# Selection in the first and last pass of a graph network kernel: selectors against a PSUM column, and in the last pass message forming shared between VectorE and ScalarE

## The reference, cut to what matters

```
x = layernorm(x + L0(x))   # (1+eps)*x + segment_sum(relu(x[src] + edge_attr), dst)
x = layernorm(x + L1(x))   # two rounds of segment_sum(w * x[dst], src), w = dinv[src]*dinv[dst]
x = layernorm(x + L2(x))   # two graph convolutions: segment_sum(x[src], dst) @ w_rel + x @ w_root + b
x = layernorm(x + L3(x))   # relu(segment_sum(edge_weight * (x @ w)[src], dst) + b)
```

## Time and profile before

| | us |
|---|---|
| median of three runs | 9893.8 (9879.71 to 9897.39) |
| the profiled execution, its device time | 9887.35 |
| the profiled execution, its span | 9885.6 |
| VectorE busy | 7177.8 (73%) |
| TensorE matmul busy | 7068.5 (72%) |
| GpSimd busy | 4237.3 (43%) |
| ScalarE busy | 3856.5 (39%) |

### The profile page before, as it was taken

One profiled execution on the slowest core, in us unless ns is written; L12 is line 12 of the kernel. 1 busy time (PEld: TensorE's weight loads), 2 busy tenths in 40 slices (PEclk: granted clock), 3 DMA queues, 4 the chain that ended last, 5 costly groups with the idle time before them and its releaser, 6 DMA issues.

```text
span 9885.6 us, 235117 instructions
## 1 busy us (share of the span) xinstructions
PE 7068.5 (72%) x71829; PEld 5632.3 (57%) x71830; DVE 7177.8 (73%) x13458; ACT 3856.5 (39%) x11229; POOL 4237.3 (43%) x3907
## 2 busy tenths in 40 slices
PE   9888887878821778985666566656676666677987
PEld 8665555556611667883346335533564345566887
DVE  6655555555545778998888888888887888777996
ACT  0355555555522675435840683068206830000000
POOL 0477777777731662003630562056204620465000
PEclk9855555565555555556889788878887889555555
DMA  9466666653367996445888788868876888355442
GB/s 331 125 179 179 178 191 180 182 139 79 79 191 253 301 312 191 111 108 183 306 293 281 252 304 292 267 233 304 293 251 216 304 291 269 128 194 187 112 108 68
DMA packets 1133195, 2087.05 MB, mean 211 GB/s; under 512 B 391662, under 2 KB 655086, under 8 KB 1132590
## 3 DMA queue, kind: packets, MB, share of 16 engines
q1 hardware_dynamic: 812062, 1195.55, 41.9%
q0 software_dynamic: 219008, 627.65, 16.5%
q10 hardware_dynamic: 101904, 261.43, 7.9%
HBM read 1191.46 MB, written 892.68 MB: 211 GB/s over the span
## 4 chain that ended last, share of the span: by engine, by line
DVE 28%; issue 25%; DMA 15%; PE 14%; POOL 13%; DVEq 3%; ACT 2%; POOLq 0%; SPq 0%; ACTq 0%
POOL edge_rows L470 13%; DVE WORK L1097 7%; PE psum L818 5%; DMA WORK<-parts_by_slot 5%; DMA BIG<-edge_rows 5%; DVE WORK L1163 4%; DVE BIG L1148 4%; DVE WORK L1158 3%; PE psum L699 3%; DVE WORK L907 3%; DMA WORK<-blocks_by_edge 3%; DMA edge_rows<-WORK 2%; DVE WORK L1099 2%; ACT WORK L627 2%; PE psum L813 1%
## 5 line engine op out<-in xcount | busy, mean ns | idle before, releaser
L497 POOL DMA_INDIRECT messages_in_parts<-WORK,goal x1480 | 1437.3, 971 | 2756.8 <-ACT WORK L627 2435.7
L470 POOL DMA_INDIRECT edge_rows<-WORK x1664 | 1959.9, 1178 | 863.0 <-issue 491.1
L627 ACT CAST WORK<-psum 128x432 bf16<-128x432 f32 (+1 forms) x4440 | 1707.1, 1019 | 872.2 <-PE psum L813 872.0
L813 PE MATMUL psum<-BIG,WORK 128*128 x11840 | 1357.9, 245 | 874.3 <-DVE WORK L1097 393.9
L1097 DVE TENSOR_TENSOR WORK<-WORK,psum 128x1024 bf16<-128x1024 uint8 x1480 | 1690.3, 1213 | 358.2 <-PE psum L813 268.2
L813 PEld LDWEIGHTS psum<-BIG,WORK 128*128 128x128 bf16 x11840 | 806.8, 106 | 1425.2 <-issue 1108.2
L907 DVE TENSOR_TENSOR WORK<-lane_k,slot_part 128x1024 bf16<-128x1024 bf16 x2220 | 1509.5, 680 | 8.6 <-PE psum L813 8.6
L841 PE MATMUL psum<-WORK 128*128 128x144 bf16 x11840 | 1081.9, 246 | 513.5 <-DVE WORK L907 459.6
L504 POOL DMA_INDIRECT whole_messages<-BIG,goal x740 | 832.0, 1124 | 1248.6 <-DVE BIG L1111 622.1
L841 PEld LDWEIGHTS psum<-WORK 128*128 128x128 bf16 x11840 | 939.0, 149 | 656.6 <-issue 348.2
L818 PE MATMUL psum<-BIG,WORK 128*128 x17760 | 958.6, 214 | 388.9 <-issue 204.4
(11 more groups left out here) (175 smaller groups left out, 8490.0 us busy)
## 6 DMA issues: line engine op xcount, KB each, us to landing
WORK<-messages_in_parts SPq DMA_DIRECT2D x1480, 288.0 KB, 4.2
WORK<-parts_by_slot SPq DMA_DIRECT2D x444, 640.0 KB
BIG<-edge_rows SPq DMA_DIRECT2D x148, 1040.0 KB, 7.2
BIG<-whole_messages SPq DMA_DIRECT2D x740, 193.5 KB, 2.4
messages_in_parts<-BIG ACTq DMA_DIRECT2D x37, 2880.0 KB
WORK<-blocks_by_edge SPq DMA_DIRECT2D x416, 256.0 KB
edge_rows<-BIG ACTq DMA_DIRECT2D x1, 76960.0 KB, 244.4
whole_messages<-BIG ACTq DMA_DIRECT2D x37, 1920.0 KB
```

Source lines behind the costliest of these rows:

```text
L470: pool.indirect_dma_start(rows_dram, bass.IndirectOffsetOnAxis(ap=at_stage[g][:, j:j + 1], axis=0), row_buf[g][:, j, :], None).then_inc(s_ ...
L497: pool.indirect_dma_start(unit_dram, bass.IndirectOffsetOnAxis(ap=goal[1 - d][:, t:t + 1], axis=0), msg[c].rearrange("p k f -> p (k f)"), ...
L627: act.copy(msg[c][:, 3 * b:3 * b + w, :].rearrange("p k f -> p (k f)"), spread_bank(c, 3 * b)[:, 0:w * W3]).then_inc(s_staged[b], 1)
L813: m = pe.matmul(o, select[c % GB][:, k, :], V3[:, ds(b * W3, W3)], start=True, stop=True)
```

## The change: what it does

- `selector` uses in all six passes the tensor_tensor with the PSUM column that the plain passes had; the copy of `here` into that column stands before every selection.
- In the weight pass the products of a batch go to two PSUM banks, slots 0 to 3 in one and slots 4 to 7 in the other (`half_bank`); batches alternate between two such pairs. Before, a batch had one bank, of five.
- In the weight pass ScalarE forms slots 0 to 3 with four multiplications of 128x48, each with its slot's weight as a scalar per partition (`form_first`, semaphore `s_zside`), and VectorE forms slots 4 to 7 with one tensor_tensor of 128x192.
- GpSimd's scatter in the weight pass waits for both, and TensorE's batch t for both engines' forms of batch t-2.

```
+KA = 4
...
+        def half_bank(c, k):
+            return bank[2 * (c % 2) + k // KA]
...
 # GpSimd
                         pool.wait_ge(s_z, t + 1 + cut_before(q))
-                        if q == 0:
+                        if kind == "edge":
                             pool.wait_ge(s_noted, t + 1)
+                        else:
+                            pool.wait_ge(s_zside, t + 1)
...
 # ScalarE
+                def form_first(t):
+                    act.wait_ge(s_spread, t + (1 + q * BATCHES))
+                    c = t % RING
+                    act.wait_ge(s_store[c], 16 * (t // RING + PAIRS * q))
+                    for k in range(KA):
+                        m = act.mul(z[c][:, k, :], half_bank(c, 0)[:, k * D:(k + 1) * D], w_s[:, t, k:k + 1])
+                    m.then_inc(s_zside, 1)
...
+                elif kind == "weight":
+                    for t in range(BATCHES):
+                        form_first(t)
...
 # TensorE
-                        if kind != "plain":
-                            wait_past(pe, s_z, t + (cut_before(q) - (GB - 1)))
+                        if kind == "edge":
+                            wait_past(pe, s_z, t - (GB - 1))
+                        if kind == "weight":
+                            wait_past(pe, s_z, t + (cut_before(q) - 1))
+                            wait_past(pe, s_zside, t - 1)
...
+                            o = bank[c % GB][:, k * D:(k + 1) * D] if kind == "edge" else half_bank(c, k)[:, k % KA * D:(k % KA + 1) * D]
...
 # VectorE, selector
-                    if kind == "plain":
-                        m = v.tensor_tensor(SEL[c % GB], part_row[c // GB][:, c % GB, :], here_p.to_broadcast([128, T * K]), ALU.is_equal)
-                    else:
-                        m = v.tensor_scalar(SEL[c % GB], part_row[c // GB][:, c % GB, :], here[:, 0:1], None, ALU.is_equal)
-                    m.then_inc(s_sel, 1)
+                    v.tensor_tensor(SEL[c % GB], part_row[c // GB][:, c % GB, :], here_p.to_broadcast([128, T * K]), ALU.is_equal)\
+                        .then_inc(s_sel, 1)
...
 # VectorE, form in the weight pass
-                        m = v.tensor_tensor(z[c], got, w_s[:, ds(i * RING + c, 1), :].rearrange("p a k -> p (a k)")
-                                            .unsqueeze(2).to_broadcast([128, K, D]), ALU.mult)
+                        m = v.tensor_tensor(z[c][:, KA:K, :], half_bank(c, KA)[:, 0:(K - KA) * D].rearrange("p (k f) -> p k f", f=D), w_s[:, ds(i * RING + c, 1), KA:K].rearrange("p a k -> p (a k)")
+                                            .unsqueeze(2).to_broadcast([128, K - KA, D]), ALU.mult)
...
-                if kind == "plain":
-                    step(v.tensor_copy(here_p, here[:, :]))
+                step(v.tensor_copy(here_p, here[:, :]))
```

More of the change, by code:

```diff
@@ L268, in gnn_program @@
                                       sem("low_parts_ready"))
+        s_zside = sem("first_slots_formed")
         s_deg, s_dturn, s_dcopy, s_dsum = (sem("degrees_added"), sem("degrees_turned"), sem("turned_degrees_copied"),
@@ L816, in select_rows @@
                                 continue
+                            o = bank[c % GB][:, k * D:(k + 1) * D] if kind == "edge" else half_bank(c, k)[:, k % KA * D:(k % KA + 1) * D]
                             for f in range(3):
-                                m = pe.matmul(bank[c % GB][:, k * D:(k + 1) * D], select[c % GB][:, k, :],
-                                              V3[:, ds(b * W3 + f * D, D)], start=f == 0, stop=f == 2)
+                                m = pe.matmul(o, select[c % GB][:, k, :], V3[:, ds(b * W3 + f * D, D)], start=f == 0, stop=f == 2)
                         m.then_inc(s_spread, 1)
```

## The result

The changed kernel takes 10011.92 us (median of 6 runs, 9979.78 to 10030.0) against 9895.59 us (9879.71 to 9927.37) for the kernel before on the same chips: 1.0108 times as long, 95% interval 1.0082 to 1.0134. The forecast was 10004 us.

What follows compares the result with a forecast made beforehand. A loop of waits between VectorE and TensorE was taken to bound both selections; +64 us (edge) and +46 (weight) on 9887.35 us gave 9997, and 6 us for the median 10004; range 9945 to 10055 us.

Steps and rivals of the forecast that it cites:

- The bound: Edge and weight passes: a loop of waits between VectorE and TensorE, 2.93 us for two batches, 1.465 each.
- VectorE's own work: Edge pass: VectorE alone needs 0.48 + 1.15 = 1.63 us a batch, below the loop's 1.695, so the loop decides.
- The selector: Both passes: the selector costs 0.46 us more and stands in the loop; edge pass +64 us, ends +52 and +84.
- the transfers' cost: Edge pass: 32 us beyond loop and stops before the change; 0 to 32 left after it, taken as 12.
- The weight pass: Weight pass: longer selector, form 0.21 us shorter, loop 3.18 us, 1.59 a batch; +46 us, ends +18 and +85.
- ScalarE's pieces: Weight pass: four pieces of 184 to 267 ns each, costing nothing unless one takes over 0.37 us.
- TensorE's added wait: Weight pass, behind the selector's wait: its count was reached long before, so nothing; at most 0.05 us in the loop, +9 us.
- its rule: Both selections: VectorE's two-port operations lock GpSimd out of a shared port pair; the new selector sets GpSimd free.
- GpSimd in charge: Both selections: GpSimd's scatter sets the pace and gets shorter, 114 us less, 9780 us; chance 6%.
- Transfers in charge: Edge pass: transfers set the pace and hide the longer selector, +19 us there, 9959 us in all; chance 18%.
- ScalarE too slow: Weight pass: ScalarE's pieces take over 0.37 us each and set the pace, +124 us there, 10082 us; chance 8%.
- a sign of being wrong: Outside the two stages: the forecast is wrong if anything there moves by more than 10 us.

Runs made afterwards that it cites:

- the first group: Four kernels on one chip (before: 9901.05 us): new selector in edge pass alone 9950.14, weight pass alone 9976.02; changed with old selectors 9890.92, with selector waited for last 9993.71.
- the split alone: Changed kernel with the old tensor_scalar selectors put back in edge and weight passes: 9890.92 us, 0.9994 times the kernel before.

## Why the prediction was right

**The bound.** Right for the weight pass: a loop of waits between VectorE and TensorE, two batches on the way. The experiments of the first group moved that stage as the loop's terms say. In the edge pass the forecast had the loop decide at 1.695 us a batch, with VectorE's own work (1.63) below it. There VectorE's own 1.60 decides; the loop with the edge pass's own terms, 0.47 + 1.21 + 0.16 + 1.36 = 3.20 for two batches, gives the same 1.60. The form hardly waits for TensorE any more (15 times), where the forecast had these waits nearly unchanged. That the form placed later shortened both stages on three other chips supports the loop.

**The selector.** 1.214 us, as read from the plain passes. The edge pass was forecast at +64 and came at +48. The terms of the loop, 0.24 from selector to TensorE and 1.46 from there to the form, were read in the weight pass; the edge pass has 0.16 and 1.34. This error stands before and after alike and takes itself out: 369 x 1.36 = 502 before and 369 x 1.60 = 590 after are 88 us apart, and the forecast added 84. What was mis-sized is the rest, which the forecast took for the transfers' cost: 32 before, 12 left, so 20 given back. With the edge pass's own loop and 72 of stops it is 71 us before and 31 after, so 40 were given back. The waits for edge rows, 66.9 and 20.7 us, say the same. It is an estimate from single executions, good to some 5 us; that all of it is the transfers' is not shown. The clock doesn't carry it: TensorE had the higher level for 31 us of this stage before and for none after, but for 61 us in the kernel with the split alone, whose edge selection was the longest of the three with the old selector.

**The weight pass.** Forecast +46, measured +67. The form of 192 elements took 0.356 us (0.350 forecast), ScalarE's pieces 0.302, beyond the bound of 0.267 taken from its nearest rows and the "near 0.2" that was to show it, but below the 0.37 at which they would count. What was mis-sized is TensorE's added wait: nothing was given to it and 0.05 us at most, and it cost 0.10 in the loop, 18 of the missing 21 us. The run with the selector waited for last shows it: 28.7 us came back with no wait removed. The reasoning that a count reached long before costs nothing overlooked that the instruction which carries the wait has to be executed behind the one that is late.

**The rivals.** GpSimd in charge (6%) is out: its scatter became 0.13 to 0.18 us shorter, as its rule says, and nobody waited for it; the split alone left it at 1152 ns and was the faster kernel. Transfers in charge (18%) is out for +19 us, since the edge pass lost 48; but some 40 of the loop's 88 us were hidden there, by the estimate above. ScalarE too slow (8%) is out by 0.302. The sum came out closer than its parts, +115 for +110, because one was 16 too high and the other 21 too low: that is luck. The forecast also named as a sign of being wrong that anything outside the two stages moves by more than 10 us. The stretch ahead moved by 14; but that stretch, with the same code, moves by up to 18 over these kernels, so the sign was set too tight.

## What to carry to other kernels

When two engines hand batches to each other and neither is full, add up the loop from the timeline and divide by the batches on the way: an operation's price is its share of that loop, whatever the busy shares say, until one engine's own work for a batch is longer. Read the loop's terms in the very stage that is asked about. An operation that frees another engine is worth nothing where nobody waits for that engine. Waits whose counts are sums of a loop register cost an instruction each, so put the one that comes last in time last; and a step that only has to be done some time should stand several places later in the program than what it waits for.

## What the runs showed of the hardware

- On TensorE's queue each wait that needs an addition behind the late wait adds 0.08 to 0.10 us: 0.16 us from selector to matmul with none, 0.24 with one, 0.34 with two.
- ScalarE's multiplication of 128x48 from PSUM with a scalar per partition takes 302 ns, and four in a row 0.88 us; its cast of 128x128 from PSUM takes 267.
- VectorE's tensor_scalar from uint8 in SBUF lengthens GpSimd's indirect DMA beside it from 970 to between 1098 and 1152 ns; the tensor_tensor with a PSUM column doesn't.
- The kernels took 9 to 10% longer on three other chips. In code that is the same, the matmuls of a batch ran as closely as on the first chips, but VectorE's form started 1.86 to 2.35 us (medians) after the batch's first matmul instead of 1.47. Its cause was not found.
